# Expert layer and second attention in one block, with the first batch opened early and each output projection deferred into the next batch

## The chip, the cores and the metric

One core of a Trainium2 chip runs the whole program. The metric is the device time of one execution in microseconds (us). A matmul runs on TensorE (PE, with PEld for its weight loads), elementwise work on VectorE (DVE), ScalarE (ACT) and GpSimd (POOL). SyncE (SP) issues almost all DMAs; POOL issues the scatter, the stores of the experts' results and the gather.

## The reference, cut to what matters

Four sublayers stand in a row on x of 4 x 512 rows of 256 columns: cross attention, a layer of 8 experts of which each token uses one, a second cross attention with 16 heads of 64 and 128 memory slots, and a quantized feed-forward part. The two in the middle are the ones touched:

```python
x = x + ffn0(layernorm(x))       # idx = argmax(x @ Wr + br); out = gate * (gelu(x W1[idx] + b1) W2[idx] + b2)
x = x + xattn1(layernorm(x), ctx, ctx)
# q = x wq + bq; k = [ctx wk + bk ; mk]; v = [ctx wv + bv ; mv], 16 heads of 64, 512 + 128 keys
# out = concat(softmax(q k^T / 8) v) wo + bo
```

Keys and values come from `ctx` and from the memory `mk`, `mv` alone. Only the queries need the experts' result.

## The kernel before, in words

`build` runs four stages one after the other: `attention0`, `mixture`, `attention1`, `feed_forward1`. Each is a block with one instruction list for each engine; the next block begins when all engines have ended. `x_all` (4 batches x 4 tiles of 128 rows) stays in SBUF throughout. The weights of the second attention (`Attention1Weights`, seven arrays, `wo` among them) are loaded by SP inside `attention0` and held.

**mixture.** DVE measures and scales the rows (`measure`, `scale_rows`), with the inverse deviation taken by POOL (L819); PE transposes them and scores them against `wr`; a chain of small DVE steps turns the scores into a slot for each token and an owner (expert) for each tile of 256 slots. POOL scatters the 16 tiles to `x_slots` in HBM (L833), SP clears that array first (L768) and loads the weights of the first three tiles. Then 15 tiles run in 5 turns over a ring of 3 (L1003, L1014, L1023 on PE, L868 on ACT, L952 and L957 on DVE, L838 stores on POOL). At the end POOL waits for the last store and gathers the 16 tiles back (L842), and DVE adds each to `x_all` (L962).

**attention1.** Setting up: POOL fills constants (L1233 to L1239), DVE splits the memory keys into a high and a low fp32r part (`hi`, `lo`, L1346 and L1348), SP copies these to `mem_hl` and `mem_h1` (L1192) and loads `ctx_t` (L1222). Then the opening of batch 0: `begin_norm`, `end_norm` and `turned_rows` make the transposed normalized rows `xn_t`; for the first three pairs of heads (BRING = 3) a query and a key projection (L1534) go through ACT (`hi`, L1289) and DVE (`lo`, `split`, L1393), and SP stacks them with six DMAs a pair (`stack`, L1202) into `q_hh`, `q_lm`, `k_hl`, `k_h1`. `hi` and `lo` have one buffer for queries and one for keys, so pair p + 1 is written only after all six DMAs of pair p have landed. Values follow (L1543, L1384), and for two pairs (RANK = 2) the row maxima of the scores: ten fills of `p_m` reduced by DVE (L1402, L1405), one transposition, `neg_max` (L1418), and a small DMA (L1208).

Then a loop runs `turn(b, True)` for batches 0 to 2, and `turn(3, False)` stands behind it. A turn has 8 pairs, each with 5 key tiles. PE's order is written out in `STEPS`: scores of the tile (L1579, L1580), a projection or value of a later pair, maxima of the pair after next, `times_v` of the tile before (L1594), `total` (L1605) of the pair before. POOL adds the tiles of probabilities (L1260), and DVE takes the reciprocal of the totals (L1426) and normalizes (L1429, `norm_ready`). After pair 7 the turn ends with its last `times_v`, `total` and `normalize`, and four output projections of 16 matmuls each (L1646), each added by DVE to `x_all` (L1465).

## Time and profile before

| | us |
|---|---|
| median of the runs | 1827.51 (1823.39 to 1827.77) |
| the profiled execution | 1828.99 |
| its span, first to last instruction | 1827.3 |
| PE busy | 1501.3 (82% of the span) |
| DVE / ACT / POOL busy | 903.3 / 496.4 / 451.6 |

The stages end at about 481 (first attention), 818 (experts), 1666 (second attention) and 1827 (feed-forward) us of the span. The profiled execution took 1.7 us more than its span and 1.5 us more than the median. A row of the timeline gives the start and the length of an instruction or of a merged run of like ones, its engine and line, what it writes and reads, and in brackets how long its engine sat idle before it and what ended that. "x4" is the number merged.

### The profile page before, as it was taken

How to read it: one execution, taken by the hardware profiler on the slowest of the kernel's cores; microseconds unless marked ns; L12 is line 12 of the kernel's file. 1: busy time of each engine (PE TensorE's matmuls, PEld its weight loads, DVE VectorE, ACT ScalarE, POOL GpSimd, SP SyncE). 2: the span in 40 equal slices, each digit the busy share in tenths (PEclk: the TensorE clock that was granted, in tenths of full speed). 3: DMA queues.
4: the chain of work that ended last, by engine and by line, in shares of the span. 5: the costliest groups of instructions: out<-in, count | busy, mean ns of one | idle time of the engine just before them, and what ended most of it. 6: DMA issues, size and time to landing. Idle time of an engine off the chain costs nothing. (4 is left out here: it accounts for less than half of the span.)

```text
span 1827.3 us, 19385 instructions
## 1 busy us (share of the span) xinstructions
PE 1501.3 (82%) x6088; PEld 889.5 (49%) x6088; DVE 903.3 (49%) x1684; ACT 496.4 (27%) x620; POOL 451.6 (25%) x261
## 2 busy tenths in 40 slices
PE   5888888889619999922599989998899979996996
PEld 2334343343518777721345445444544454435785
DVE  5566566656410000012357654776366635656566
ACT  2433324325102222200033322333133313330221
POOL 2000000000130000041034442445144514471333
PEclk8899899999759999966699989999899989996998
DMA  6523113220253544225556634555256625502001
GB/s 158 143 35 39 26 17 46 35 36 1 87 210 121 181 154 164 110 79 79 72 72 81 92 46 62 76 81 69 35 73 94 83 35 73 69 1 95 1 1 46
DMA packets 62234, 136.08 MB, mean 74 GB/s; under 512 B 10592, under 2 KB 21216, under 8 KB 57568
## 3 DMA queue, kind: packets, MB, share of 16 engines
q1 hardware_dynamic: 59440, 127.26, 37.1%
q0 software_dynamic: 2736, 8.13, 1.3%
q8 instruction: 26, 0.43, 0.1%
q14 instruction: 32, 0.26, 0.1%
HBM read 58.55 MB, written 12.06 MB: 39 GB/s over the span
## 5 line engine op out<-in xcount | busy, mean ns | idle before, releaser
L1260 POOL TENSOR_TENSOR a_probs<-a_probs 128x1024 f32<-128x1024 f32 x128 | 305.1, 2384 | 476.7 <-PE a_p_o L1594 475.7
L1299 ACT ACTIVATE a_probs<-a_p_s 128x1024 f32<-128x1024 f32 x160 | 163.9, 1024 | 332.0 <-PE a_p_s L1580 331.9
L417 DVE CUSTOM_DVE_ANT_0 a_scratch<-a_p_m,a_bias_q 128x512 bf16<-128x512 f32 x256 | 163.8, 687 | 121.0 <-PE a_p_m L572 121.0
L1402 DVE TENSOR_REDUCE a_max_ctx<-a_p_m 128x1 f32<-128x512 f32 x256 | 169.3, 688 | 77.0 <-PE a_p_m L1555 73.7
L327 ACT ACTIVATE a_probs<-a_p_s 128x1024 f32<-128x1024 f32 x128 | 130.7, 1025 | 178.8 <-PE a_p_s L597 178.3
L595 PE MATMUL a_p_s<-a_q_stack,a_k_stack 128*128 128x512 f32 x256 | 121.7, 502 | 31.2 <-DMA a_q_stack<-a_neg_max 31.2
L572 PE MATMUL a_p_m<-a_k_stack,a_q_stack 127*128 127x512 f32 x256 | 130.4, 555 | 13.9 <-DVE a_mx L417 7.0
L1594 PE MATMUL a_p_o<-a_probs,a_v 128*64 128x512 f32 x512 | 138.7, 620 | 0.0
L1014 PE MATMUL e_p_h<-e_rows_t,e_w 128*128 128x256 f32 x480 | 123.1, 390 | 13.8 <-DVE e_rows_t L952 13.8
L1426 DVE RECIPROCAL a_recip<-a_p_sum 128x512 f32<-128x512 f32 x32 | 106.9, 3339 | 29.3 <-PE a_p_sum L1605 29.3
L1023 PE MATMUL e_p_y<-e_w,e_hidden 128*128 128x256 f32 x480 | 118.6, 380 | 0.6 <-ACT e_hidden L868 0.6
L1579 PE MATMUL a_p_s<-a_q_hh,a_k_hl 128*128 128x512 f32 x256 | 118.6, 463 | 0.0
L957 DVE TENSOR_TENSOR e_y<-e_p_y,e_b 128x512 f32<-128x512 f32 x15 | 10.4, 692 | 218.2 <-PE e_p_y L1023 218.2
L1555 PE MATMUL a_p_m<-a_k_hl,a_q_hh 128*128 128x512 f32 x256 | 106.3, 465 | 10.3 <-DVE a_v L1384 8.8
L1014 PEld LDWEIGHTS e_p_h<-e_rows_t,e_w 128*128 128x128 f32 x480 | 92.2, 195 | 30.1 <-DVE e_rows_t L952 17.6
L597 PE MATMUL a_p_s<-a_bias_k,a_ident_b 128*128 128x512 bf16 x256 | 104.5, 408 | 0.0
L1580 PE MATMUL a_p_s<-a_q_lm,a_k_h 65*128 65x512 f32 x256 | 101.9, 398 | 0.0
L1393 DVE SCALAR_TENSOR_TENSOR a_lo<-a_p_m,a_bqk,a_hi 128x512 fp32r<-128x512 f32 x64 | 47.4, 747 | 107.0 <-ACT a_hi L1289 107.0
L1023 PEld LDWEIGHTS e_p_y<-e_w,e_hidden 128*128 128x128 f32 x480 | 91.0, 190 | 14.1 <-ACT e_hidden L868 1.8
L868 ACT ACTIVATE e_hidden<-e_p_h,e_b 128x256 f32<-128x256 f32 x120 | 56.1, 474 | 150.0 <-PE e_p_h L1014 149.9
L1289 ACT ACTIVATE a_hi<-a_p_m,a_bqk 128x512 fp32r<-128x512 f32 x64 | 43.8, 687 | 193.8 <-PE a_p_m L1534 166.4
L1555 PEld LDWEIGHTS a_p_m<-a_k_hl,a_q_hh 128*128 128x128 f32 x256 | 45.3, 191 | 98.2 <-DVE a_max_ctx L1402 52.7
(198 smaller groups left out, 2183.9 us busy)
## 6 DMA issues: line engine op xcount, KB each, us to landing
e_w<-in_L_w SPq DMA_DIRECT2D x30, 1024.0 KB, 8.2
a_q_hh<-a_hi SPq DMA_DIRECT2D x64, 256.0 KB, 5.5
a_q_lm<-a_lo SPq DMA_DIRECT2D x32, 256.0 KB, 6.9
a_k_hl<-a_hi SPq DMA_DIRECT2D x32, 256.0 KB, 7.7
a_k_hl<-a_lo SPq DMA_DIRECT2D x32, 256.0 KB, 9.1
a_k_h<-a_hi SPq DMA_DIRECT2D x32, 256.0 KB, 10.3
a_ctx_t<-in_ctx_t SPq DMA_DIRECT2D x8, 512.0 KB, 5.7
a_q_stack<-a_hi SPq DMA_DIRECT2D x32, 128.0 KB, 5.6
```

Source lines behind the costliest of these rows:

```text
L327: act.activation(probs[:, j % 4, :, :], p_s[:, j % 2, :, :], ACT.Exp).then_inc(exp_done.sem, 1)
L417: dve.tensor_tensor_reduce(scratch[:, fill.n % M_BANKS, :], m, bias_q[:, i % NT, :], 1.0, -3.0e38, ALU.add, ALU.max, mx[:, i:i + 1]).then_ ...
L572: done(pe.matmul(m, q_stack[0:MAX_ROW, h, P * t:P * (t + 1)], k_stack[0:MAX_ROW, h, :], start=True, stop=True))
L595: pe.matmul(p_s[:, slot, i, :], k_stack[:, h, P * kt:P * (kt + 1)], q_stack[:, h, :], start=True, stop=False)
L1014: mm = pe.matmul(p_h[:, c % 4, 0:CT], w1[:, r, k, P * c:P * (c + 1)], rows_t[:, r % 2, k, :], start=(k == 0), stop=(k == DC - 1))
L1023: mm = pe.matmul(p_y[:, t, 0:D], hidden[:, d % 4, P * t:P * (t + 1)], w2[:, r, d, :], start=(d == 0), stop=(d == FC - 1))
L1260: pool.tensor_tensor(probs[:, kt], probs[:, kt - 1], probs[:, kt], ALU.add)\
L1299: act.activation(probs[:, kt, :, :], p_s[:, (KT1 * p + kt) % 2, :, :], ACT.Exp).then_inc(exp_done.sem, 1)
L1402: dve.tensor_reduce(max_ctx[:, NT * head + t:NT * head + t + 1], m, AX, ALU.max)\
L1555: done(pe.matmul(m, q_hh[:, s, P * t:P * (t + 1)], k_hl[:, s, :], start=True, stop=True))
L1579: pe.matmul(p_s[:, n % 2, i, :], first, q_hh[:, s, :], start=True, stop=False)
L1594: mm = pe.matmul(p_o[DK * i:DK * (i + 1), :], vh, probs[:, kt, i, :], start=(kt == 0), stop=(kt == KT1 - 1))
```

## The change

`mixture` and `attention1` become one block, `mixture_attention1`, with shared SBUF and PSUM.

- Memory keys, `mem_v` and `ctx_t` of batch 0 are loaded at the block's start. DVE splits the memory keys after the routing and before the tile loop, and SP copies them behind the loads of the first rows. POOL fills `mem_h1` among its first constants, and `k_h1` after the scatter.
- The opening follows a list, `OPENING`: three keys with values between them, then the rows of batch 0, then queries and maxima. A key uses buffer 1 of `hi` and `lo`, a query buffer 0 or 1, and each has three DMAs to wait for and not six. `combine(0)` on DVE stands behind the third key's split; `combine(1)` to `combine(3)` stand beside the queries. POOL inverts the deviation of batch 0 between gather 8 and gather 9.
- The space of the experts' weights is used for `q_hh`, `k_hl` and `q_lm`. `wo` lies in the experts' result buffer, so it is loaded behind the opening, and PE waits for it ahead of the first turn. `Attention1Weights` loads six arrays.
- A turn no longer ends with its output. `times_v`, `total` and `normalize` of pair 7 stand in pair 0 of the next turn, and the four output projections (`out`) in pair 1, one ahead of each of the key tiles 1 to 4. ACT reads the output of a pair into `o_raw` (two buffers) and waits for `norm_ready` before it. The first turn is written out, the loop runs batches 1 and 2, and the last turn ends as before.

```diff
-    LOADS = 16 * 7
+    LOADS = 16 * 6
...
+        with ExitStack() as until_experts_end:
+            w1, w2 = (until_experts_end.enter_context(nc.sbuf_tensor("a1_" + name, shape, F32))
+                      for name, shape in (("w1", [P, RING, DC, FF]), ("w2", [P, RING, FC, D])))
+        q_hh = sb("q_hh", [P, 2 * HELD, S], F32R)
+        k_hl = sb("k_hl", [P, 2 * HELD, S], F32R)
+        q_lm = sb("q_lm", [ROWS, 2 * HELD, S], F32R)
...
+        STEPS = (("query", "score", "score", "key", "times_v"),
+                 ("out", "score", "score", "value", "maximum", "maximum", "times_v", "maximum"),
+                 ("out", "maximum", "score", "score", "maximum", "value", "times_v", "maximum"),
+                 ("out", "maximum", "score", "score", "maximum", "times_v", "maximum", "rows"),
+                 ("out", "maximum", "total", "score", "turn", "score", "times_v"))
...
+                if what == "out" and (p != 1 or not behind):
+                    continue
...
+        OPENING = (("key", 0), ("values", 0), ("key", 1), ("values", 1), ("key", 2), ("rows", 0), ("query", 0), ("query", 1),
+                   ("maxima", 0), ("query", 2), ("maxima", 1))
...
         def _(sp):
+            for dst, src in ((xn_t[:].rearrange("p c n -> p (c n)"), A["L1_mk"]), (mem_v[:], A["L1_mv"])):
+                sp.dma_start(dst, src).then_inc(loaded, 16)
+            sp.dma_start(ctx_t[:], A["ctx_t"][0]).then_inc(ctx_in.sem, 16)
...
+            sp.wait_ge(prep, 3)
+            sp.wait_ge(filled_s, 1)
+            for dst, part in ((mem_hl[0:DK], hi), (mem_hl[DK:P], lo), (mem_h1[0:DK], hi)):
+                sp.dma_start(dst.rearrange("p i a n -> p i (a n)").bitcast(F32),
+                             part[:].rearrange("p a n -> p (a n)").bitcast(F32)).then_inc(mem_in, 16)
             with sp.Fori(0, TURNS - 1) as i:
...
+            for p in range(BRING):
+                split_ready.wait(sp, -1, 2 * PAIRS + p + 1)
+                stack_key(p, 1, k_first)
+            for p in range(BRING):
+                split_ready.wait(sp, -1, 2 * PAIRS + BRING + p + 1)
+                stack_query(p, p % 2, q_first[p])
+                if p:
+                    bring_maxima(-1, PAIRS + p - 1)
+            sp.wait_ge(y_stored.sem, 16 * TILES)
+            sp.dma_start(wo, A["L1_wo"]).then_inc(wo_in, 16)
+            turn(0, True)
+            with sp.Fori(1, B - 1) as b:
+                turn(b, True)
+            turn(B - 1, False)
...
         def _(pool):
+            pool.memset(mem_h1[:].bitcast(F32), 1.0).then_inc(filled_s, 1)
             pool.memset(ends[:], 0.0).then_inc(e_filled, 1)
...
+            pool.wait_ge(scattered, 16 * N_TILES)
+            pool.memset(k_h1[:].bitcast(F32), 1.0).then_inc(filled_s, 1)
...
             pool.wait_ge(y_stored.sem, 16 * TILES)
             for t in range(N_TILES):
+                if t == 2 * NT:
+                    invert_deviation(-1)
                 pool.indirect_dma_start(out=back[:, t, :], out_offset=None, in_=A["y_slots"],
...
         def _(act):
+            def read_output(b, p):
+                pv_done.wait(act, b, KT1 * (p + 1))
+                norm_ready.wait(act, b, p - 1)
+                act.activation(o_raw[:, p % 2, :], p_o[:], ACT.Copy).then_inc(o_read.sem, 1)
...
         def _(dve):
+            dve.tensor_scalar(bqk[:, 0, :], bqk[:, 0, :], DK ** -0.5, None, ALU.mult).then_inc(bqk_ready, 1)
+            dve.tensor_scalar(wq[:], wq[:], DK ** -0.5, None, ALU.mult).then_inc(scaled, 1)
+            dve.tensor_copy(flat(hi), flat(xn_t)).then_inc(prep, 1)
+            dve.wait_ge(prep, 1)
+            dve.tensor_tensor(flat(lo), flat(xn_t), flat(hi).bitcast(F32), ALU.subtract).then_inc(prep, 2)
             with dve.Fori(0, TURNS) as i:
...
+            for what, p in OPENING:
+                if what == "key":
+                    open_split(1, p, 1, p, (k_first, 16 * 3 * p) if p else None)
+                elif what == "values":
+                    values(-1, fill, 4, p)
+                elif what == "rows":
+                    combine(0)
+                    dve.wait_ge(combined, NT)
+                    begin_norm(-1)
+                    end_norm(-1)
+                    turned_rows(-1, fill)
+                elif what == "query":
+                    open_split(0, p, p % 2, BRING + p,
+                               ((k_first, 16 * 3 * BRING) if p == 1 else (q_first[p - 2], 16 * 3)) if p else None)
+                    if p == 0:
+                        combine(1)
+                    elif p == 1:
+                        combine(2)
+                        combine(3)
+                        dve.wait_ge(combined, N_TILES)
...
         def _(pe):
+            def project_out(b, banks, t):
+                m = banks.free()
+                if t == 0:
+                    norm_ready.wait(pe, b, 0)
+                for p in range(PAIRS):
+                    mm = pe.matmul(m[:, 0:D], o_norm[:, p, P * t:P * (t + 1)], wo[:, p, :],
+                                   start=(p == 0), stop=(p == PAIRS - 1))
+                done(mm)
...
+            pe.wait_ge(wo_in, 16)
+            turn(0, True, False)
+            with pe.Fori(1, B - 1) as b:
+                turn(b, True, True)
+            turn(B - 1, False, True)
```

## Rows read from the trace of the kernel before

**Rows 1.** Windows: stretch, its us, busy us by engine (instructions), granted clock, DMA share, GB/s

```profile
560.00:789.80 229.80, 210.16 (x970) 180.00 (x968) 18.42 (x28) 57.99 (x117) 10.13 (x14) 0.99 0.42 146
789.70:912.30 122.60, 36.69 (x83) 18.86 (x82) 35.30 (x70) 3.91 (x6) 25.69 (x25) 0.61 0.51 84
1080.60:1107.20 26.60, 17.68 (x70) 13.47 (x68) 7.51 (x8) 0.60 (x1) 3.85 (x2) 0.81 0.00 1
1107.20:1273.50 166.30, 161.68 (x620) 81.53 (x620) 107.89 (x150) 57.18 (x64) 75.58 (x33) 1.00 0.59 79
1273.50:1300.50 27.00, 18.05 (x69) 14.29 (x69) 7.43 (x8) 0.60 (x1) 3.77 (x2) 0.81 0.00 0
1466.70:1493.00 26.30, 17.47 (x70) 13.38 (x68) 7.47 (x8) 0.60 (x1) 3.81 (x2) 0.81 0.00 0
```

**Rows 2.** Timeline, from the last expert tile to the memory keys' landing

```profile
789.87 0.69 DVE L957 TENSOR_TENSOR e_y<-e_p_y,e_b 128x512 f32<-128x512 f32 x1 [14.26 <-PE e_p_y L1023]
794.03 1.04 POOL L842 DMA_INDIRECT e_back<-y_slots,e_slot  x1 [2.08 <-DMA y_slots<-e_y]
800.69 1.67 DVE L962 SCALAR_TENSOR_TENSOR x_all<-e_back,e_gate,x_all 128x256 f32<-128x256 f32 x4 [10.12 <-DMA e_back<-y_slots,e_slot]
813.43 0.95 POOL L842 DMA_INDIRECT e_back<-y_slots,e_slot  x1 [0.30 <-issue]
822.26 1.80 POOL L1237 MEMSET a_mem_h<- 65x2048 f32 x1
843.53 1.40 DVE L1355 BATCH_NORM_STATS2 a_stats<-x_all 128x6 f32<-128x256 f32 x4 [15.71 <-DMA a_mem_h<-a_hi]
```

**Rows 3.** Timeline, the opening of batch 0

```profile
856.65 1.18 SPq L1202 DMA_DIRECT2D a_q_hh<-a_hi  x2
870.60 1.27 ACT L1289 ACTIVATE a_hi<-a_p_m,a_bqk 128x512 fp32r<-128x512 f32 x2 [12.99 <-DMA a_k_h<-a_hi]
872.10 1.18 SPq L1202 DMA_DIRECT2D a_q_hh<-a_hi  x2
902.78 10.20 SPq L1208 DMA_DIRECT2D a_q_lm<-a_neg_max  x2
912.32 3.78 PE L1534 MATMUL a_p_m<-a_xn_t,a_wq 128*128 128x512 f32 x4 [0.37 <-DVE a_neg_max L1418]
```

**Rows 4.** DMAs issued in 855 to 870: KB each, median us to landing

```profile
a_q_hh<-a_hi SPq DMA_DIRECT2D x2, 256.0 KB, 4.9
a_q_lm<-a_lo SPq DMA_DIRECT2D x1, 256.0 KB, 6.9
```

**Rows 5.** The same for the held weights, issued in 40 to 60

```profile
a_wq<-in_L_wq SPq DMA_DIRECT2D x1, 1024.0 KB, 4.9
a_wo<-in_L_wo SPq DMA_DIRECT2D x1, 1024.0 KB, 11.1
```

**Rows 6.** Timeline, the end of batch 0's turn

```profile
1084.66 1.98 PE L1605 MATMUL a_p_sum<-a_probs,a_ones 128*64 128x512 f32 x4 [3.98 <-POOL a_probs L1260]
1090.92 15.62 PE L1646 MATMUL a_p_m<-a_wo,a_o_norm 128*128 128x256 f32 x64 [4.28 <-DVE a_o_norm L1429]
1099.78 0.42 DVE L1465 TENSOR_TENSOR x_all<-x_all,a_p_m 128x256 f32 x1 [3.01 <-PE a_p_m L1646]
1103.23 0.42 DVE L1465 TENSOR_TENSOR x_all<-x_all,a_p_m 128x256 f32 x1 [3.03 <-PE a_p_m L1646]
```

**Rows 7.** Timeline, pairs 0 to 2 of batch 0

```profile
938.60 1.88 PE L1534 MATMUL a_p_m<-a_ctx_t,a_wk 128*128 128x512 f32 x4
942.15 0.53 SPq L1202 DMA_DIRECT2D a_k_hl<-a_hi  x1
950.70 1.08 PE L1605 MATMUL a_p_sum<-a_probs,a_ones 128*64 128x512 f32 x4
956.46 0.78 DVE L1429 TENSOR_TENSOR a_o_norm<-a_o_norm,a_recip 128x512 f32<-128x512 f32 x1
959.85 0.60 ACT L1303 ACTIVATE a_o_norm<-a_p_o 128x512 f32<-128x512 f32 x1 [0.20 <-PE a_p_o L1594]
```

More of the change, by code:

```diff
@@ new lines, in mixture_attention1, with steps @@
+        PER_MAX = 2 * (NT + 1)
+        def steps(p, kt, ahead, behind):
+            for what in STEPS[kt]:
+                if what == "value" and (p % 2 or p == PAIRS - 2 and not ahead):
+                    continue
+                if what == "rows" and (p != PAIRS - 4 or not ahead):
+                    continue
+                if what == "out" and (p != 1 or not behind):
+                    continue
+                if not ahead and (what in ("query", "key") and p + BRING >= PAIRS
+                                  or what in ("maximum", "turn") and p + RANK >= PAIRS):
+                    continue
+                yield what
@@ new lines, in mixture_attention1, with fills @@
+        FILLS = {"query": 1, "key": 1, "maximum": 1, "turn": 1, "value": 1, "rows": NT, "out": 1}
+        DVE_FILLS = {"maximum": 1, "value": 1, "rows": NT, "out": 1}
+        def fills(kinds, last_p=PAIRS - 1, last_kt=KT1 - 1):
+            return sum(kinds.get(w, 0) for p in range(last_p + 1) for kt in range(KT1)
+                       if p < last_p or kt <= last_kt for w in steps(p, kt, True, True))
+        BEFORE = NT + 2 * BRING + 2 + RANK * (PER_MAX + 1)
+        DVE_BEFORE = NT + 2 + RANK * PER_MAX
@@ L1309, in turn @@
                         heads = 0
-                        for what in steps(p, kt, ahead):
+                        for what in steps(p, kt, ahead, behind):
                             if what in ("query", "key"):
@@ L1321, in turn @@
                                     exps(b, p, kt)
[L1322 removed]
+                            elif what == "times_v" and kt == 0 and (p or behind):
                                 read_output(b, p - 1)
[L1324 to L1332 removed]
@@ L1333, in _, with open_project @@
-            with act.Fori(0, B - 1) as b:
-                turn(b, True)
-            turn(B - 1, False)
+                if not ahead:
+                    read_output(b, PAIRS - 1)
+            def open_project(n, p, at, freed):
+                if freed:
+                    act.wait_ge(*freed)
+                m = fill.bank()
+                m_full.wait(act, -1, fill.n)
+                act.activation(hi[:, at, :], m, ACT.Identity, bias=bqk[:, n, p:p + 1]).then_inc(hi_ready.sem, 1)
+            act.wait_ge(held.loaded, held.LOADS)
@@ L1616, in turn @@
                         head = 0
-                        for what in steps(p, kt, ahead):
+                        for what in steps(p, kt, ahead, behind):
                             if what in ("query", "key"):
```

943 lines of the change are left out of this document (452 added, 491 removed).

## The prediction

> **What bounds the kernel now.** I read the windows first, by stage. In the experts' stretch PE works 210.2 of 229.8 us, in a turn of the second attention 161.7 of 166.3, and the stretches between them are different [rows 1]: from the last expert tile to the first turn 122.6 us pass with 36.7 us of PE work, at a mean granted clock of 0.61, and at the end of each of the first three turns some 27 us pass at 0.81. Both are a mix of its two levels, 1.2 and 2.4 GHz, and PE had been idle before it fell. So PE is the bound while it is fed, and these four stretches are chains of single steps. The change touches just these.
>
> The timeline shows what the first chain is made of [rows 2]: the last result of the experts ends at 790.6; the gathers go from 794.0 to 814.4; the memory keys are prepared behind them, and DVE waits 15.7 us for their copies, until 843.5. In the opening [rows 3] the first stack is issued at 856.65 and the second pair's ACT step starts at 870.60, released by a DMA; the third pair repeats it. The first maxima leave at 902.8, and turn 0 starts at 912.3. At the end of a turn [rows 6] PE waits 4.0 us for POOL's sum and 4.3 us for DVE's normalization, then projects 64 times.
>
> **The opening, worked out.** All times are on the clock of the profiled span, on the old course up to 790.6.
>
> Removed from the path: constants, the memory keys' split and their copies (they go under the routing's and the experts' slack: DVE was idle over 200 us of the tile loop, and DMA engines were busy 42% there [rows 1]). If that cover is gone, the worst is the old price, 15.7 us of copying [rows 2].
>
> Added: a chain of three key stacks. A key takes from its projection to its first stack DMA 938.60 to 942.15 = 3.55 us in a warm turn [rows 7]. So stack 0 is issued at 794.2. How long do three DMAs of 256 KB take? The third of a stack of six was issued 1.2 us after the first [rows 3] and landed 6.9 us later [rows 4]: 8.1 us. Two rows bound it: the first DMAs alone, 4.9 us [rows 4], and the full six, 856.65 to 870.60 = 13.95 us [rows 3]. I take 8.1, from the row of the same size, and 1.7 more for stack 0, as the first eight gathers run beside it (an estimate: they held the DMA engines about 30%, of the 5.7 us or so in which the stack's data moves). From a landing to the next stack's issue the trace has 870.60 to 872.10 = 1.5 us [rows 3]. So stack 0 lands at 804.0, stack 1 is issued at 805.5 and lands at 813.6, and stack 2 is issued at 815.1. The values between them are hidden by these waits.
>
> `combine(0)` stands behind the third split on DVE, though batch 0's rows are back by 800.7 [rows 2]. It takes 1.67 and ends at 816.8. From `begin_norm` to the first stack's issue the old trace has 843.53 to 856.65 = 13.1 us [rows 2, 3], so query 0 is issued at 829.9 and lands at 838.0; stack 2 (landed at 823.2) is covered. POOL waits in front of gather 8 for the statistics, until 819; a pow and eight gathers at (813.43 - 794.03) / 15 = 1.29 us [rows 2] bring it to 831, and `combine(3)` is over by 837. That is still under query 0's landing, with about 1 us to spare.
>
> Maxima 0 take 902.78 to 912.32 = 9.5 us [rows 3], until 847.5. Query 2 stands between the maxima: four projections at the low clock take 3.8 us, as in the row of 912.32 [rows 3], and 3.55 - 1.88 = 1.7 for ACT, DVE and hand-overs [rows 7], until 853.0. Maxima 1 end at 862.5. Now a new wait: SP issues `wo` only behind this, at about 863.2, and PE stands in front of turn 0 until it has landed; everything is queued behind PE there. A megabyte from HBM landed in 4.9 us as the first of its group and in 11.1 us as the fourth [rows 5]. SP's queue holds nothing large at this time, so I take 4.9; nothing would be the lower end, 11.1 the upper. Turn 0 starts at 868.1, where it was 912.3 [rows 3]: **-44.2 us**.
>
> The Trainium skill, "DMA: Bandwidth & Descriptors", section "Anatomy of one DMA — SWDGE (gpsimd) path", has a fit of 2.0 us and the bytes at 436 GB/s (taken on POOL's queue); by it 768 KB in one go would be 3.8 us and not 8.1. The trace speaks against it for these copies within SBUF [rows 4]; what it would give is one of the rivals.
>
> **The turns' ends.** Between the turns lie 26.6, 27.0 and 26.3 us [rows 1], 79.9 in all. In the new order the total and the 64 matmuls remain, in a stretch where PE is never idle: the total is 1.1 us at full clock [rows 7], 16 matmuls take 1103.23 - 1099.78 = 3.45 [rows 6], so 4 x 3.45 + 1.1 = 14.9 a batch and 44.7 for three. **-35.2 us.** The last turn ends as before. Is the work that hid nothing now a new wait? `out` at the head of tile 1 of pair 1 needs the normalization of pair 7, which will stand where pair 0's does in pair 1's last tile: over at 956.46 + 0.78 = 957.2, while the next pair's tile 1 begins about when ACT reads the output, 959.85 [rows 7]: 2.6 us of slack. ACT's new wait in front of `o_raw` has the same 2.6 us. DVE gets four adds of 0.42 and one normalization more a batch and is 65% busy in the turns (107.9 of 166.3 us [rows 1]), so it follows.
>
> **Smaller parts.** POOL's `mem_h1` fill, 1.8 us [rows 2], stands ahead of the first pow (L819), with which a serial chain to the scatter begins: **+1.8 us**, bounds 0 and 1.8. Three more loads ahead of the clearing (1.5 MB) end long before the scatter. `k_h1`'s 3.5 us on POOL fall between scatter and first store, where POOL sat idle over 20 us. `wo` missing in the first attention: nobody there waited for those loads, 0. The first turn written out adds code to fetch; the old last turn, also written out, began with no longer stretch before it than the others (26.3 against 26.6 and 27.0 [rows 1]), so 0, and up to 3 if it shows.
>
> **Sum.** 1829.0 - 44.2 - 35.2 + 1.8 = 1751.4 for the profiled execution. This one stood 1.5 above the median, so I forecast **1750 us** for the median, with its own range of 1738 to 1766.
>
> **The rivals.**
> A. The stacks are not shorter for being three: the landing is paid by a queue's depth of latency, at 13.95. Four such steps lie on the path, 4 x (13.95 - 8.1) = +23 us: 1773. For it: PE, ACT and DVE never waited less than that for a stack in the old opening. Against: within the six, landings came one behind the other (4.9 us for the first, 6.9 for the third [rows 4]).
> B. Three DMAs move as one: with the 4.9 us of the first ones [rows 4] as the whole stack's price it is 4 x 3.2 = -13 us: 1737. By the fit of the Trainium skill's page above it would be 4 x (8.1 - 3.8) = -17 us, 1733.
> C. The change doesn't do what it says: the overlap of the opening holds, but `out` between tiles stalls PE (a bank of `p_m` read late by DVE, or the normalization late), and 30 of the 35 us come back: 1780. For it: DVE's reciprocal of 3.3 us stands in the way once a pair. Against: 2.6 us of slack.
> D. Slower than before: ACT's new wait for `norm_ready` makes ACT, DVE and PE wait in a ring in every pair. It decides if the normalization is more than the 2.6 us late [rows 7]; the gain of 77.6 us is used up when each of 32 pairs is 2.4 us longer, that is with a normalization 5.0 us later than now, and slower by over 0.3% from 5.2 us on. At 5.6 us late: 32 x 3.0 = 96 us, 1846. Against: DVE has a third of its time free, so no backlog can build up.
>
> **How the numbers follow.** Forecast 0.72, A 0.10, B 0.07, C 0.08, D 0.03. With the bounds of the unknown costs (stacks from -13 to +23, `wo` from -4.9 to +6.2) the range is 1732 to 1776: 18 below the forecast for the stacks' and `wo`'s lower bounds, 26 above for the stacks' upper one and part of `wo`'s. It holds the forecast, A and B and leaves out C and D. A measurement of this kernel can tell 0.3% (5.5 us) from no change. Faster by more than that: all but D, 0.96; within: 0.02; slower: 0.02.
>
> **What would show each step.** In the profile after: the first memory-key copies before 560 us; key stacks 10 to 11 us apart after the experts; gather 8 idle on a DVE release at about 819; a wait of PE for `wo` of about 5 us ahead of turn 0; turn 0 starting 42 us earlier; no stretch of 27 us between turns, only at the last one; `out` matmuls with 3.45 us for 16 and no idle time before them; turn starts 166.3 + 14.9 = 181 us apart. The prediction is wrong if the stacks land more than 12 us after issue, if PE idles before `out`, or if the 166.3 us of a turn [rows 1] grow.

## The result and the profile after

The changed kernel takes 1746.4 us (median of four runs, 1743.57 to 1749.67), the kernel before 1826.6 beside it: a ratio of 0.956, 95% interval 0.954 to 0.959. The profiled execution spans 1747.0 us, against 1827.3. One run of mem_late (4532 us) and one of recip2 (2921 us) lie far above all others, for no cause that a trace shows, and are left out of every number below.

Three stretches of its windows, in the columns of [rows 1]: the opening, from the experts' last result to turn 0, then turn 0 (no outputs to project), turn 1 and turn 2 (each with the outputs of the batch before).

```profile
790.06:867.10 77.04, 38.01 (x82) 18.73 (x82) 33.99 (x66) 4.12 (x6) 19.64 (x19) 0.62 0.59 106
867.15:1035.72 168.57, 163.09 (x616) 82.88 (x616) 107.81 (x150) 57.27 (x64) 74.34 (x32) 0.98 0.60 79
1035.72:1215.48 179.76, 176.54 (x691) 94.02 (x689) 114.57 (x158) 56.64 (x65) 78.98 (x34) 1.00 0.57 74
1215.48:1398.60 183.12, 178.49 (x691) 94.96 (x689) 114.46 (x158) 56.72 (x65) 78.99 (x34) 0.99 0.56 72
```

The opening is 77.1 us long where it was 121.8 (from 790.56 to 912.32 in [rows 2, 3]); PE's work in it is about the same (38.0 us for 36.7), and so is its granted clock (0.62 for 0.61). Turns 1 and 2 are 179.8 and 183.1 us long; in the kernel before, a turn and the stretch behind it took 193 [rows 1]. PE is busy for 98 and 97% of these two.

The steps of the opening in the timeline, to be read against [rows 2, 3]; PE L1692 projects, SPq is the issue of a DMA, L1287 is `combine`, L1048 POOL's inversion, L1080 a gather:

```profile
790.54 1.96 PE L1692 MATMUL a_p_m<-a_ctx_t,a_wk 128*128 128x512 f32 x4 [1.30 <-DVE a_yb L1281]
794.23 0.58 SPq L960 DMA_DIRECT2D a_k_hl<-a_hi  x1
803.24 0.69 ACT L1169 ACTIVATE a_hi<-a_p_m,a_bqk 128x512 fp32r<-128x512 f32 x1 [9.94 <-DMA a_k_h<-a_hi]
804.81 0.53 SPq L960 DMA_DIRECT2D a_k_hl<-a_hi  x1
812.87 0.69 ACT L1169 ACTIVATE a_hi<-a_p_m,a_bqk 128x512 fp32r<-128x512 f32 x1 [8.94 <-DMA a_k_h<-a_hi]
814.33 1.66 DVE L1287 SCALAR_TENSOR_TENSOR x_all<-a_probs,a_gate,x_all 128x256 f32<-128x256 f32 x4
818.20 1.04 POOL L1048 TENSOR_TENSOR a_rstd<-a_rstd,a_minus_half 128x4 f32<-128x4 f32 x1 [14.26 <-DVE a_rstd L1301]
819.44 1.14 POOL L1080 DMA_INDIRECT a_probs<-y_slots,a_slot  x1 [0.20 <-issue]
828.88 1.18 SPq L955 DMA_DIRECT2D a_q_hh<-a_hi  x2
837.28 1.19 PE L1587 MATMUL a_p_m<-a_k_hl,a_q_hh 128*128 128x512 f32 x2 [7.67 <-DMA a_q_lm<-a_lo]
847.46 0.79 SPq L973 DMA_DIRECT2D a_q_lm<-a_neg_max  x1
862.17 0.43 SPq L997 DMA_DIRECT2D a_yb<-in_L_wo  x1
867.15 3.78 PE L1562 MATMUL a_p_m<-a_xn_t,a_wq 128*128 128x512 f32 x4 [6.06 <-DMA a_yb<-in_L_wo]
```

Each bracket is one term of the prediction's sum: the key stacks land after 9.0 and 8.1 us, `combine(0)` comes directly behind the third split (which starts at 813.66), gather 8 at 819.44 behind the inversion, the last maxima at 861.43, and PE then waits for `wo`.

At the last turn's end the two old waits of [rows 6] still stand (waits of PE: us in total, times, longest). In the turns, the 192 `out` matmuls of three batches have no idle time in front of them (group of L1644: busy us, mean ns, idle before):

```profile
PE a_p_m L1644 <- DVE a_o_norm L1371: 4.3, 1, 4.3
PE a_p_os L1636 <- POOL a_probs L1063: 4.1, 1, 4.1
L1644 PE MATMUL a_p_m<-a_yb,a_o_norm 128*128 128x256 f32 x192 | 43.7, 381 | 0.0
```

Where the 80.3 us between the two profiled executions went, span against span:

| Stretch | before | after | difference |
|---|---|---|---|
| first attention | 481.7 | 478.6 | -3.0 |
| routing and experts | 308.9 | 311.4 | +2.5 |
| opening | 121.8 | 77.1 | -44.7 |
| turn 0 to the end of attention | 753.8 | 717.5 | -36.3 |
| last block | 161.2 | 162.3 | +1.1 |

POOL's fill of `mem_h1` (below) is 1.8 of the experts' 2.5, and the other 0.7 seems to go with it: in best and best_pow_early, which fill later, this stretch is 309.0 and 308.9 us long; through which step is not shown.

The first attention differs by one load, that of `wo`. Its largest single difference lies just behind these loads, where PE waits for a copy of row maxima that SP issues after them. Before the change and after it:

```profile
70.73 0.79 PE L595 MATMUL a_p_s<-a_q_stack,a_k_stack 128*128 128x512 f32 x1 [6.82 <-DMA a_q_stack<-a_neg_max]
68.19 0.79 PE L595 MATMUL a_p_s<-a_q_stack,a_k_stack 128*128 128x512 f32 x1 [4.08 <-DMA a_q_stack<-a_neg_max]
```

In the other eleven kernels, all without this load, the wait is 3.5 to 5.6 us. So most of the 3.0 us probably belongs to the change; how much is not shown, since there is one profile of the kernel before. The rest of this stretch scatters: among the kernels without the load it ended between 474.6 and 480.7, and a median of a few runs carries about as much of it. Below, a kernel's opening is therefore read from its profile and its time from the runs.

### The profile page after: what moved, and what is told of

It reads as the page before. It is cut to its first block and busy times, and to the rows that moved or that the text cites. A ratio compares the mean times of both kernels' runs of the same rounds, so it can differ in the third digit from the quotient of the medians.

```text
span 1747.0 us, 18982 instructions
## 1 busy us (share of the span) xinstructions
PE 1492.1 (85%) x6088; PEld 884.1 (51%) x6088; DVE 904.9 (52%) x1684; ACT 494.4 (28%) x618; POOL 450.9 (26%) x257
## 5 line engine op out<-in xcount | busy, mean ns | idle before, releaser
L572 PE MATMUL a_p_m<-a_k_stack,a_q_stack 127*128 127x512 f32 x256 | 130.4, 555 | 13.6 <-DVE a_mx L417 7.0
L1626 PE MATMUL a_p_os<-a_probs,a_v 128*64 128x512 f32 x512 | 138.1, 618 | 0.0
L1507 PE MATMUL a_p_s<-a_o_raw,a_w 128*128 128x256 f32 x480 | 124.0, 393 | 13.8 <-DVE a_o_raw L1276 13.8
L1587 PE MATMUL a_p_m<-a_k_hl,a_q_hh 128*128 128x512 f32 x256 | 111.1, 481 | 18.3 <-DVE a_v L1323 8.1
L1281 DVE TENSOR_TENSOR a_yb<-a_p_os,a_yb 128x512 f32<-128x512 f32 x15 | 10.4, 691 | 219.1 <-PE a_p_os L1516 219.1
L1516 PE MATMUL a_p_os<-a_w,a_probs 128*128 128x256 f32 x480 | 118.6, 380 | 0.6 <-ACT a_probs L1111 0.6
L1368 DVE RECIPROCAL a_recip<-a_p_os 128x512 f32<-128x512 f32 x32 | 106.8, 3337 | 17.3 <-PE a_p_os L1636 17.3
L1507 PEld LDWEIGHTS a_p_s<-a_o_raw,a_w 128*128 128x128 f32 x480 | 92.8, 196 | 30.4 <-DVE a_o_raw L1276 17.6
L1111 ACT ACTIVATE a_probs<-a_p_s,a_b 128x256 f32<-128x256 f32 x120 | 55.9, 473 | 150.7 <-PE a_p_s L1507 150.7
L1516 PEld LDWEIGHTS a_p_os<-a_w,a_probs 128*128 128x128 f32 x480 | 91.1, 190 | 14.1 <-ACT a_probs L1111 1.8
L572 PEld LDWEIGHTS a_p_m<-a_k_stack,a_q_stack 127*128 127x128 f32 x256 | 49.0, 206 | 69.2 <-DVE a_mx L417 43.9
L608 PE MATMUL a_p_o<-a_probs,a_v 128*32 128x512 f32 x512 | 73.7, 650 | 5.4 <-ACT a_probs L327 5.4
## 6 DMA issues: line engine op xcount, KB each, us to landing
a_k_h<-a_hi SPq DMA_DIRECT2D x32, 256.0 KB, 10.6
```

The source lines that it names most:

```text
L572: done(pe.matmul(m, q_stack[0:MAX_ROW, h, P * t:P * (t + 1)], k_stack[0:MAX_ROW, h, :], start=True, stop=True))
L1507: mm = pe.matmul(p_h[:, c % 4, 0:CT], w1[:, r, k, P * c:P * (c + 1)], rows_t[:, r % 2, k, :], start=(k == 0), stop=(k == DC - 1))
L1516: mm = pe.matmul(p_y[:, t, 0:D], hidden[:, d % 4, P * t:P * (t + 1)], w2[:, r, d, :], start=(d == 0), stop=(d == FC - 1))
L1587: done(pe.matmul(m, q_hh[:, s, P * t:P * (t + 1)], k_hl[:, s, :], start=True, stop=True))
L1626: mm = pe.matmul(p_o[DK * i:DK * (i + 1), :], vh, probs[:, kt, i, :], start=(kt == 0), stop=(kt == KT1 - 1))
```

## The experiments

Each kernel was timed in three rounds (best: five) beside the kernel before, whose medians there were 1825.0, 1826.4 and 1826.6. The openings of all of them, from the profiles, divided where batch 0's statistics start. This table carries most of what follows:

| Kernel | experts' end to statistics | statistics to turn 0 | opening | time, us |
|---|---|---|---|---|
| before | 53.0 | 68.8 | 121.8 | 1826.6 |
| changed | 26.0 | 51.1 | 77.1 | 1746.4 |
| own_tail | 25.7 | 51.3 | 77.0 | 1781.0 |
| mem_late | 44.3 | 51.1 | 95.4 | 1760.3 |
| gathers_first | 30.7 | 50.4 | 81.1 | 1747.2 |
| k_late | 12.4 | 62.2 | 74.6 | 1740.1 |
| wo_hidden | 25.7 | 45.9 | 71.6 | 1737.4 |
| free_half | 18.7 | 50.0 | 68.7 | 1735.8 |
| rows_first | 18.7 | 54.6 | 73.3 | 1738.8 |
| best | 18.7 | 41.0 | 59.7 | 1724.5 |
| best_pow_early | 18.8 | 49.8 | 68.5 | 1730.1 |

**own_tail: the outputs at each turn's end again.**

```diff
-                if what == "out" and (p != 1 or not behind):
+                if what == "out":
...
+                times_v(b, PAIRS - 1, KT1 - 1)
+                total(b, PAIRS - 1)
+                for t in range(NT):
+                    project_out(b, banks, t)
```

> The changed kernel with one part undone: every batch projects its outputs at its own end again, and the opening stays new. My theory (the deferral is worth 35 us, all of it at three turn ends, and PE's work in between is unchanged): turn 0 starts at about 867 as in the changed kernel, the stretches between turns are 26 to 27 us again, and the time is 1746.4 + 35 = 1781. Rival (part of the deferral's gain was given back inside the turns, because the 64 extra matmuls of a batch disturb the banks of p_m): the turns without them are shorter by more than 10.8 us of matmul time each against the 181 us of the changed kernel's turns, and the time is 1770 or less. Rival 2 (the opening brought less than its 45 us once the tails are back): over 1790.

1781.0 us, ratio 0.975 (0.974 to 0.977): 34.6 more, as expected. The waits of [rows 6] are back at all four ends (waits of PE: total, times, longest):

```profile
PE a_p_m L1642 <- DVE a_o_norm L1370: 17.2, 4, 4.3
PE a_p_os L1634 <- POOL a_probs L1063: 16.2, 4, 4.1
```

The starts of PE's query projections give the length of each pair, and these show what the deferral changed (us, pairs 0 to 7 of turn 1):

```
own_tail  21.45 18.30 22.68 18.36 24.81 18.32 22.68 46.14
changed   22.68 31.93 22.69 18.31 24.82 18.33 22.68 18.32
```

27.8 us leave the last pair, 13.6 come into pair 1, 1.2 into pair 0, and the other five are equal to 0.05. Nothing was given back inside the turns: the first rival falls. The opening is unchanged (77.0 us), so the two parts add up.

**mem_late: the memory keys behind the experts again.**

```diff
+            dve.tensor_copy(flat(hi), flat(xn_t)).then_inc(prep, 1)
+            dve.wait_ge(prep, 1)
+            dve.tensor_tensor(flat(lo), flat(xn_t), flat(hi).bitcast(F32), ALU.subtract).then_inc(prep, 2)
             dve.wait_ge(mem_in, 16 * 3)
             fill = Fill(PER - BASE)
```

The lines come from ahead of the tile loop, and the three copies on SP move behind it, too.

> The changed kernel with one part undone: the memory keys are split into hi and lo and copied by their three DMAs (1.5 MB) only when the experts have ended, ahead of key 0, where the changed kernel does it under the experts. My theory (this part alone was worth its old price, and nothing behind it has room to make it good): two DVE operations of about 1.1 us each and the 15.7 us of copying that the trace of before shows stand ahead of key 0, the gathers run beside them and not beside stack 0 (1 us back); turn 0 starts 16 to 18 us later, time 1763. Rival (with the memory keys on the path the gathers are done early and combine(0) is no longer late, or the copies share the time with the gathers): less than 10 us, 1756 or lower.

1760.3 us, ratio 0.965 (0.962 to 0.967), 13.9 more by the runs; its opening is 18.3 longer. In its profile the first attention is 4.0 us shorter than in the changed kernel's, turn 2 and the last block 1.1 each and turn 0 0.7, all out of the edit's reach. All of the 18.3 is ahead of the statistics, and nothing behind them is shorter:

```profile
786.83 1.23 DVE L1425 TENSOR_TENSOR a_lo<-a_xn_t,a_hi 128x1024 fp32r<-128x1024 f32 x1
804.27 3.75 PE L1691 MATMUL a_p_m<-a_ctx_t,a_wk 128*128 128x512 f32 x4 [18.96 <-DMA a_mem_h<-a_hi]
```

PE waits 19.0 us, then projects at the low level (3.75 us for what takes 1.96 above). By the opening, this part of the change is worth a little more than the 15.7 us of copying alone.

**gathers_first: all sixteen gathers and four combines ahead of the statistics.**

```diff
             for t in range(N_TILES):
-                if t == 2 * NT:
-                    invert_deviation(-1)
                 pool.indirect_dma_start(...)
+            invert_deviation(-1)
```

> The changed kernel with all sixteen gathers ahead of POOL's inversion and all four batches combined ahead of batch 0's statistics, the keys still first. It asks what gathering batch 0 first is worth in this order of work. Theory 1 (combine(0) waits for the third key split until 814.3, when the last gather has been issued, too; only the three further combines of 1.66 us stand ahead of the statistics): the gathers' last landing is at about 817 to 818, the statistics start 5 to 7 us later, and the three combines leave the place behind query 0, where nothing waited for them: 1751.5 to 1753.5. Theory 2 (the gathers beside the key stacks land late, as in free_half, where one took 10.2 us in the median): the last lands after 822, 10 us or more later: 1757 or more.

1747.2 us, ratio 0.957 (0.955 to 0.959): 0.8 more by the runs, 4.0 in the opening (its first attention is 2.9 us shorter). The statistics start 4.7 us later, somewhat under the 5 to 7 of theory 1. With the keys in front, gathering batch 0 first brings only the time of the further combines: the gathers were done while DVE waited for the key stacks.

**k_late: rows, query and key in the old order.**

```diff
-        OPENING = (key 0, values 0, key 1, values 1, key 2, rows, query 0, query 1, maxima 0, ...)
+        OPENING = (rows, query 0, key 0, query 1, key 1, query 2, key 2, values 0, values 1, maxima 0, 1)
```

Every stack has a semaphore of its own here, as in free_half below.

> The changed kernel with the opening in the old order: batch 0's rows, then query and key of pair 0, 1 and 2, the values and the maxima; memory keys early, batch 0 gathered first and the deferred outputs stay. It asks what splitting the keys ahead of the rows is worth. Theory 1 (they were free: their stacks lay beside the gathers and the norm): without stacks beside them the gathers of batch 0 have landed at 800.7, combine(0) starts there instead of 814.3, and the first query's stack is issued at 814; from it to turn 0 the old order takes 55.7 us (856.65 to 912.32 in the trace of before), and 6 for wo: turn 0 at 876, 8 to 9 us later than the changed kernel's, time 1755. Theory 2 (the early keys are worth the three landings of 8.1 us that leave the chain, 24 us): 1770. Theory 3 (they cost as much as they bring, since they hold combine(0) back by 13.6 us): 1746.

1740.1 us, ratio 0.954 (0.952 to 0.956): 6.3 *less* than the changed kernel; 2.5 of it in the opening (the rest is in the last section). None of the three theories has it. Statistics start 12.4 us after the experts, as theory 1 says. But from there the old order no longer takes the 68.8 us of the kernel before; it takes 62.2 with `wo`, and 56.7 without the 5.5 us that `wo` is worth by wo_hidden below:

```profile
799.71 1.67 DVE L1289 SCALAR_TENSOR_TENSOR x_all<-a_probs,a_gate,x_all 128x256 f32<-128x256 f32 x4 [10.74 <-DMA a_probs<-y_slots,a_slot]
814.47 1.22 SPq L957 DMA_DIRECT2D a_q_hh<-a_hi  x2
823.68 1.18 SPq L957 DMA_DIRECT2D a_q_hh<-a_hi  x2
834.01 1.18 SPq L957 DMA_DIRECT2D a_q_hh<-a_hi  x2
822.11 0.69 ACT L1171 ACTIVATE a_hi<-a_p_m,a_bqk 128x512 fp32r<-128x512 f32 x1 [6.61 <-DMA a_q_lm<-a_lo]
826.75 0.69 ACT L1171 ACTIVATE a_hi<-a_p_m,a_bqk 128x512 fp32r<-128x512 f32 x1 [3.95 <-DMA a_k_h<-a_hi]
```

In the kernel before, the next pair waited until all six DMAs of a pair had landed, and the stacks of two pairs stood 15.45 and 15.6 us apart [rows 3]. Here each half of `hi` and `lo` has its own semaphore, query 1 is released by query 0's stack alone (landed 7.6 us after its issue) and the stacks of two pairs stand 9.2 and 10.3 us apart. These two distances are 11.5 us shorter, nearly all of the 12.1 us that the old order gained from the statistics to turn 0; no run undoes the semaphores alone. That is the gain which I had put down to early keys. The early keys themselves cost 2.5 us as the changed kernel places them: their three landings hold `combine(0)` back by 13.6 us and take 11.1 us out of what follows. With the idle half used (free_half below) the opening with early keys is 5.9 us shorter than this one.

**wo_hidden: the wait for `wo` behind turn 0.**

```diff
-            pe.wait_ge(wo_in, 16)
             turn(0, True, False)
+            pe.wait_ge(wo_in, 16)
```

> The changed kernel with PE's wait for wo moved from in front of turn 0 to behind it (turn 0 does not use wo). My theory: PE waited 6.06 us there for nothing but this load, so turn 0 starts 5 to 6 us earlier, at about 862, and the time is 1740.5 to 1741.5. Rival: the last maxima's copy (issued at 861.43, landing about 2 us later) is what turn 0 needs next, so PE stops at the first score; only 2 to 4 us come back, 1743. Rival 2: the load of 1 MB is then in flight beside the first stacks of turn 0 and takes the gain back there: 1746.

1737.4 us, ratio 0.952 (0.950 to 0.954): 9.0 less. The opening is 5.5 us shorter, which is the theory; PE starts turn 0 0.37 us behind the last maxima. The rest lies elsewhere: in its profile the first attention is 2.1 us shorter than the changed kernel's, turn 0 0.7, turn 2 1.3 and the last block 2.6.

**free_half: key 1 in the idle half.**

```diff
+        AT = {key 0: 1, key 1: 0, key 2: 1, query 0: 0, query 1: 1, query 2: 0}
+        k_first = [sem(f"k_first{p}") for p in range(BRING)]
```

AT names the half of `hi` and `lo` that a projection uses; before, all keys used 1.

> The changed kernel with key 1 of the opening written into the idle half of hi and lo (key 0 keeps the other), each stack with a semaphore of its own; order of work unchanged. So stack 1 is issued at about 798 beside stack 0 instead of behind its landing at 803, and only key 2 waits for a landing. My theory (the landing is a latency and a rate that two stacks share only in part; combine(0) is late only because it stands behind the third split on DVE): stack 0 lands at 803 to 806, combine(0) starts at 807 to 809 instead of 814.3, turn 0 starts 5 to 8 us earlier, time 1739 to 1741. Rival A of the prediction (a stack's price is the depth of what is queued, 13.95 us for six DMAs): stack 0 lands at 808 as the second stands behind it, and 3 us are left: 1743. Rival (stacks share the DMA engines fully, so that three in a row cost the same however they are issued): stack 2 lands at 822 as before, but combine(0) still comes 8 us earlier, as it needs no third stack.

1735.8 us, ratio 0.950 (0.948 to 0.953): 10.6 less, 8.4 in the opening. Stack 0 lands as before although stack 1 is issued 3.5 us behind it, so rival A is out for this place. The bound is a new one: `combine(0)` now waits for its rows.

```profile
803.25 0.69 ACT L1171 ACTIVATE a_hi<-a_p_m,a_bqk 128x512 fp32r<-128x512 f32 x1 [6.02 <-DMA a_k_h<-a_hi]
807.37 1.67 DVE L1289 SCALAR_TENSOR_TENSOR x_all<-a_probs,a_gate,x_all 128x256 f32<-128x256 f32 x4 [2.58 <-DMA a_probs<-y_slots,a_slot]
```

And the medians from issue to landing in the opening (KB each, us) say why: of the changed kernel,

```profile
a_k_h<-a_hi SPq DMA_DIRECT2D x3, 256.0 KB, 6.8
a_probs<-y_slots,a_slot POOLq DMA_INDIRECT x16, 3.9
```

and of free_half:

```profile
a_k_h<-a_hi SPq DMA_DIRECT2D x3, 256.0 KB, 11.8
a_probs<-y_slots,a_slot POOLq DMA_INDIRECT x16, 10.2
```

The third DMA of a key stack takes 11.8 us in place of 6.8, a gather 10.2 in place of 3.9. Stacks and gathers share the DMA engines; issuing more at once moves the wait, it doesn't remove it.

**rows_first: batch 0's rows and query 0 ahead of key 2.**

```diff
-        OPENING = (key 0, values 0, key 1, values 1, key 2, rows, query 0, query 1, maxima 0, query 2, maxima 1)
+        OPENING = (key 0, values 0, key 1, values 1, rows, query 0, key 2, query 1, maxima 0, query 2, maxima 1)
```

> As free_half, and in the opening batch 0's rows and query 0 stand ahead of key 2: key 0, values, key 1, values, rows, query 0, key 2, query 1, maxima 0, query 2, maxima 1. My theory (the opening of the changed kernel is bound by the order on DVE, not by the gathers or by DMA): combine(0) starts as soon as batch 0's rows are there, at 801 to 802, POOL's inversion follows its eighth gather at about 805, query 0's stack is issued at about 816 and lands at 824, maxima 0 end at 835, maxima 1 at 849, turn 0 starts at 854.5 instead of 867.15: 1734. Rival (the six stacks are bound by the DMA engines): the stacks of query 0, key 2 and query 1, issued within 10 us, land at 14 us each, query 0 at 830; turn 0 at 861 or later: 1740 or more. Rival 2: the gathers of batches 1 to 3, which now run beside these stacks, delay them by some us more.

1738.8 us, ratio 0.952 (0.951 to 0.954), and 73.3 us of opening, where I had expected 64.5. Two steps of the expectation failed:

```profile
806.20 1.67 DVE L1289 SCALAR_TENSOR_TENSOR x_all<-a_probs,a_gate,x_all 128x256 f32<-128x256 f32 x4 [8.45 <-DMA a_probs<-y_slots,a_slot]
830.22 0.75 DVE L1424 SCALAR_TENSOR_TENSOR a_lo<-a_p_m,a_bqk,a_hi 128x512 fp32r<-128x512 f32 x1 [4.40 <-ACT a_hi L1171]
834.92 1.39 PE L1587 MATMUL a_p_m<-a_k_hl,a_q_hh 128*128 128x512 f32 x2 [3.09 <-DVE a_max_ctx L1346]
```

The rows landed 16.5 us after key 0's start, as in free_half and not at 11 (the DMA engines again). And query 1's split waits on DVE for query 0's stack until 830.2, with `combine(2)` and `combine(3)` (3.25 us) behind it and the maxima behind these: PE does two of them from 829.5 on and then waits 3.1 us for a bank.

**recip2 and dose_part: how much room has the normalization?** The reciprocal of each pair is taken twice; dose_part takes 320 of its 512 columns the first time.

```diff
+                dve.reciprocal(recip[:], p_sum[:]).then_inc(dosed.sem, 1)
                 dve.reciprocal(recip[:], p_sum[:]).then_inc(sum_read.sem, 1)
```

> The changed kernel with DVE's reciprocal of the sums done twice in every pair (3.35 us and a hand-over, the same values), so that each normalization is over about 3.45 us later; it doses the slack that the prediction set at 2.6 us. My theory as the prediction has it: ACT's read of the output waits for the normalization of the pair before and is 0.8 us late in each of 32 pairs, 26 us, and 3 us more at the last one: 1775. Rival (the banks of p_m, rival C's mechanism): the splits of query and key stand behind the normalization on DVE, and PE's values and maxima wait for their banks, 2 us in a pair: 1810. Rival (there is more room than 2.6 us, and DVE's idle time takes it up): only the last normalization shows, 1750.

> The changed kernel with 320 of the 512 columns of DVE's reciprocal done once more ahead of it, 2.1 us and a hand-over of 0.1 in every pair: a dose between nothing and the 3.4 us of recip2, which cost 57 us where the prediction's slack of 2.6 us gives 26. Two readings of that are left. Theory 1 (the slack is 1.5 us and that of the banks of p_m: in the changed kernel DVE's split of the query is over at 956.2 and PE's values ask for its bank at 957.8): PE is 0.6 to 0.8 us late in a pair, on DVE's lo, 19 to 26 us, and 2 more at the last normalization: 1768 to 1775. Theory 2 (the slack is 2.6 us, ACT's wait, and the rest of recip2's price was DVE's load and the lower clock after long waits): no wait of PE in a pair, 1749.

1802.3 us (56 more, ratio 0.987, 0.984 to 0.990) and 1771.8 us (25 more, 0.971, 0.969 to 0.973). By the totals, the rival of the banks wins both times. The pair lengths (turn 1, pairs 0 to 7) say otherwise:

```
changed    22.68 31.93 22.69 18.31 24.82 18.33 22.68 18.32
dose_part  22.68 32.26 22.67 22.60 27.57 18.32 22.67 18.29
recip2     23.15 33.47 23.26 25.79 31.44 19.31 23.26 19.33
```

In ordinary pairs 2.2 us late costs nothing (0.3 in pair 1, with its outputs) and 3.45 us late costs 0.5 to 1.0 (1.5 in pair 1): the slack lies between the two doses, which fits the 2.6 that the prediction set. The rest is paid in pairs 3 and 4 alone (recip2: 7.5 and 6.6 us, dose_part: 4.3 and 2.8), where the statistics and the scaling of the next batch's rows stand on DVE between the normalization and the splits. The scaling (L1307, L1308) at pair 4 of turn 0 and POOL's tile add next to it, in the changed kernel:

```profile
954.21 1.37 DVE L1307 TENSOR_SCALAR a_o_norm<-x_all,a_mean_var,a_rstd 128x256 f32<-128x256 f32 x4
956.95 2.36 POOL L1063 TENSOR_TENSOR a_probs<-a_probs 128x1024 f32<-128x1024 f32 x1 [3.21 <-PE a_p_os L1626]
```

The same in dose_part, with PE's values (L1575), which wait for the split behind the scaling:

```profile
955.84 3.42 DVE L1308 TENSOR_SCALAR a_o_norm<-x_all,a_mean_var,a_rstd 128x256 f32<-128x256 f32 x4
956.63 2.48 POOL L1064 TENSOR_TENSOR a_probs<-a_probs 128x1024 f32<-128x1024 f32 x1 [3.22 <-PE a_p_os L1630]
959.98 1.99 PE L1575 MATMUL a_p_m<-a_wv,a_ctx_t 128*128 128x256 f32 x8 [2.35 <-DVE a_lo L1337]
```

And in recip2, without POOL's line:

```profile
958.39 3.41 DVE L1308 TENSOR_SCALAR a_o_norm<-x_all,a_mean_var,a_rstd 128x256 f32<-128x256 f32 x4
962.51 3.78 PE L1575 MATMUL a_p_m<-a_wv,a_ctx_t 128*128 128x256 f32 x8 [3.55 <-DVE a_lo L1337]
```

1.37 us became 3.4. The scaling now overlaps POOL's tile add, which in the changed kernel begins after it: in both kernels one of its four operations lasts 2.4 us and ends 0.15 us behind POOL's. So a delay over 2 us at this place is about doubled. And where PE waits 3.55 us, its next step runs at the low level (3.78 us, in dose_part 1.99 after 2.35 us of waiting). Theory 1 of dose_part met its total of 1768 to 1775 with a wait of 0.6 to 0.8 in each pair, of which there is none: right by chance.

**best and best_pow_early.** best is free_half and wo_hidden, with query 2 ahead of maxima 0 and POOL's `mem_h1` fill behind its inversions; best_pow_early inverts after the fourth gather.

```diff
-        OPENING = (..., query 0, query 1, maxima 0, query 2, maxima 1)
+        OPENING = (..., query 0, query 1, query 2, maxima 0, maxima 1)
...
-                if t == 2 * NT:
+                if t == NT:
```

The last pair of lines is best_pow_early's alone.

> free_half (key 1 in the idle half of hi and lo), wo_hidden (PE waits for wo behind turn 0), query 2 of the opening ahead of maxima 0 (PE was idle there for 7 us, waiting for query 0's stack; its half is free when that has landed), and POOL's fill of mem_h1 behind its first inversions. My theory: the three savings of the opening lie one behind the other on its chain and add up, 8.4 for the free half, 5.5 for wo, 4.7 less 1.4 for query 2 (DVE's split of it stands ahead of the first maximum), and 1.8 for the fill in the routing's chain: 19 us under the changed kernel, 1727. Rival (query 2's stack, issued at the start of maxima 0, holds up nothing, but maxima 0 and 1 are bound by PE's and DVE's hand-overs at the low clock and lose what query 2 gains): 1730. Rival (a fill of 1.8 us moved is hidden by the scatter's wait for the clearing): 1729.

> As best, with POOL's inversion behind the fourth gather instead of the eighth, so that only batch 0's gathers run beside the key stacks and the other twelve start when batch 0's statistics are there. My theory (beside two stacks the DMA engines are full: in free_half a gather took 10.2 us to land in the median against 3.9 in the changed kernel, and batch 0's last landed at 807 and not at 801): the four gathers and the two stacks are done sooner, combine(0) starts 2 to 3 us earlier; 2 us under best. Rival (the twelve gathers then run beside the query stacks, hold up their landing by as much or make combine(3) late for the first maximum): 0 to 4 us over best.

best takes 1724.5 us (1718.74 to 1725.99), ratio 0.943 (0.941 to 0.945): 102 us under the kernel before and 22 under the changed one, the fastest of all. Its opening is 17.4 us shorter, where 17.2 was expected: the edits add up. The opening:

```profile
789.67:849.38 59.71, 34.83 (x82) 17.74 (x82) 34.18 (x66) 4.12 (x6) 19.64 (x19) 0.67 0.70 119
```

The fill's term can be read by itself, from the first statistics to the first scatter, in the changed kernel:

```profile
478.63 1.40 DVE L1192 BATCH_NORM_STATS2 a_e_stats<-x_all 128x6 f32<-128x256 f32 x4 [0.32 <-PEq L84]
516.97 2.05 POOL L1037 DMA_INDIRECT x_slots<-a_probs,a_slot  x1 [23.96 <-DVE a_slot L1259]
```

and in best:

```profile
480.71 1.41 DVE L1194 BATCH_NORM_STATS2 a_e_stats<-x_all 128x6 f32<-128x256 f32 x4 [0.32 <-PEq L84]
517.28 2.05 POOL L1040 DMA_INDIRECT x_slots<-a_probs,a_slot  x1 [22.08 <-DVE a_slot L1261]
```

38.34 against 36.57 us, 1.8 us; it is 36.57 in the kernel before, too (481.67 to 518.24).

best_pow_early is 5.6 us slower than best, and neither expectation's size fits. `combine(0)` starts 16.6 us behind key 0, where it was 16.5, so the four later gathers were not what held up batch 0's. And the rival's wait is larger than expected, as DVE stands at batch 3's rows for 11 us ahead of the maxima:

```profile
801.81 1.67 DVE L1289 SCALAR_TENSOR_TENSOR x_all<-a_probs,a_gate,x_all 128x256 f32<-128x256 f32 x4 [2.61 <-DMA a_probs<-y_slots,a_slot]
831.99 1.67 DVE L1289 SCALAR_TENSOR_TENSOR x_all<-a_probs,a_gate,x_all 128x256 f32<-128x256 f32 x4 [11.01 <-DMA a_probs<-y_slots,a_slot]
```

## Why the prediction was right

- **Sum.** For the median 1750 was forecast and 1746.4 came; for the profiled execution 1751.4 and 1748.7 (its span is the 1747.0). That is 80.3 less than before, where 77.6 was forecast. The largest miss is a term put at 0, the first attention ("nobody there waited for those loads"): it became 3.0 us shorter, and PE's wait behind the loads was 6.8 us before and 4.1 after; how much of this is scatter stays open. The rest nearly cancels: 0.5 in the opening and 1.1 in the turns the one way, 0.7 in the experts and 1.1 in the last block the other.
- **Opening, -44.2: measured -44.7.** Every time of the chain came within 1.1 us: query 0 issued at 828.9 (829.9 forecast), landed at 837.3 (838.0), maxima 0 at 847.5 (847.5), `wo` issued at 862.2 (863.2), turn 0 at 867.15 (868.1). The prices of the trace before held because each was used where the same step runs again in like surroundings: three DMAs as a step of their own 8.1 us (measured 8.1 and 8.4, and 9.0 beside gathers where 9.8 was forecast), hand-overs 1.5 (1.6), `wo` 4.9 (and 4.9). Two are off and cancel: maxima 0 took 10.2 us for 9.5, and query 2 behind them 4.7 for 5.5. The Trainium skill's fit in "DMA: Bandwidth & Descriptors", section "Anatomy of one DMA — SWDGE (gpsimd) path", would give 3.8 us for a stack (an estimate), less than half of what these copies take.
- **What the sum did not say** is which part earned it. Memory keys early: 18.3 (mem_late). Early keys: -2.5, a loss (k_late). Each half released by its own stack: 12.1 (k_late's 62.2 from statistics to turn 0, less 5.5 for `wo`, against 68.8), by the distances of its stacks. `wo` itself: -5.5 (wo_hidden). That leaves 22.3 for the rows' way from the experts to the statistics: twelve gathers fewer ahead of them, no constants and no end of a block. This one is by difference and was not measured by itself, and gathers_first's 4.0 is the part of it that still shows behind the early keys. 18.3 + 22.3 + 12.1 - 5.5 - 2.5 = 44.7.
- **Turns, -35.2: measured -36.3**, but made up otherwise. The mechanism is right: 13.6 + 1.2 us come in for a batch, 14.8 where 14.9 was forecast. What leaves is larger. The stretches of 26.3 to 27.0 us [rows 1] begin 1.3 us after the point where an ordinary pair of 18.3 us would be over (1061.0 + 18.3 = 1079.3, not 1080.6); by pair lengths 27.6 to 28.3 leave. That makes 39 us for three turns, of which a stall at the loop's edge took 3.4 back (below).
- **Fill, +1.8: measured 1.8** (36.57 to 38.34).
- **Code to fetch, 0 and up to 3: a stall, measured 3.4** (3.6 in gathers_first), just over the bound. I had priced it at 0 from the old last turn, where no such stall showed; the place to look was the loop's first way back, not the code written out.
- **Rivals.** A (landing 13.95) and B (4.9): the stacks landed after 8.1 to 9.0. Both were priced with four landings on the path, while the prediction's own chain passes three (stack 0, stack 1, query 0, with stack 2 covered): A would be 1768 and not 1773, B 1740 and not 1737. But A's mechanism is real once stacks are issued together, 11.8 us for the third DMA in free_half. C: no wait ahead of `out` inside the turns. D: its point, 2.6 us, fits six of eight pairs (dose_part, recip2); it left out pairs 3 and 4, where 3.45 us late already cost 14 us a turn. On the line through both doses (25 us at 2.2, 56 at 3.45) the 77.6 us of gain would be used up at 4.3 us late (an estimate), not at 5.0.
- **The margin** of `combine(3)` ahead of the maxima, forecast at 1 us, was 0.2: it was over at 837.1 (837 forecast), and query 0 had landed at 837.3. It was luck in its parts: `combine(1)` took 4.5 us and not 1.7 (below), while the gathers were over at 829.4 and not 831.

## What to carry to other kernels

Work out a reordered chain step by step with the price that each step has in the trace at the same size and with the same neighbours; then test the parts one at a time, for a sum can be right while one of its parts is a loss (here the early keys, until the idle half was used). Release each buffer by its own semaphore before changing the order of work: waiting for all six DMAs of a pair where three would do cost about 12 us of the old opening, which the new order seemed to win. When dosing a slack, read the cost by pair or tile, not as a total; it may sit in the few places where other work stands behind the same step.

## What was not expected of the hardware

**A stall of DVE at the loop's edge.** In turn 2 of the changed kernel, the loop's second pass, DVE sits idle 4.6 us in front of the splits without a release to wait for ("issue"), and PE waits and drops to the low level (3.48 us for 1.89):

```profile
1223.11 1.41 DVE L1336 SCALAR_TENSOR_TENSOR a_lo<-a_p_m,a_bqk,a_hi 128x512 fp32r<-128x512 f32 x2 [4.57 <-issue]
1223.91 3.48 PE L1571 MATMUL a_p_m<-a_wv,a_ctx_t 128*128 128x256 f32 x8 [1.63 <-DVE a_lo L1336]
```

Turn 2 is 183.1 us long where turn 1 is 179.8. In gathers_first it is 183.3, in mem_late 182.0, in wo_hidden 181.8; in free_half, k_late, rows_first, best and best_pow_early 179.7. The DMA queues of the changed kernel from 1216 to 1225 show what runs meanwhile:

```profile
q14 instruction: 3, 0.02, 0.8%
```

These are three packets of instructions, at 1218.9, 1221.3 and 1223.7. gathers_first, mem_late and wo_hidden have three such packets in the same place, and the five kernels just named without the stall have none. The Trainium skill, "Runtime: NRT & Kernel Launch", section "Instruction fetch mechanics", says that a taken branch whose target is not in the current window of the instruction memory forces a fetch before execution goes on; the place, just behind the loop's way back, and these packets agree. The trace does not say for which engine they are, and no run here shows why other kernels are spared. It makes differences of up to 3.6 us between kernels that have nothing to do with what their edits are for, as with part of k_late's and wo_hidden's gain.

**A DVE operation blocked by POOL.** `combine(1)`'s four operations took 4.50 us where `combine(0)`'s took 1.66, as POOL's bias add ran from 829.45 to 831.80:

```profile
828.77 4.50 DVE L1287 SCALAR_TENSOR_TENSOR x_all<-a_probs,a_gate,x_all 128x256 f32<-128x256 f32 x4
829.45 2.35 POOL L1054 TENSOR_TENSOR x_all<-x_all,a_bo 128x1024 f32<-128x1024 f32 x1
```

The first of the four lasts from 828.77 to 832.09, 0.3 us beyond the end of POOL's add, though by the records it began 0.7 us before it; the other three take 1.2 us together. The Trainium skill's "SBUF — State Buffer", section "Who interferes with whom", says that a DVE instruction with two SBUF inputs contends with a POOL instruction that reads SBUF, and that the port pair they share is an exclusive lock; this row agrees with it. It cost nothing here, since 0.2 us of margin was left behind `combine(3)`. In recip2 and dose_part a block that looks like it (3.4 us for 1.37) was on the path; there the DVE operation reads only one large tile, so that these two inputs do not explain it, and its cause is not shown.
